# Attention and mixture-of-experts kernel: where VectorE adds the low-rank tiles to the weights of two experts

## The reference

```python
gate = jnp.einsum('btd,edf->ebtf', x, Wg)
up = jnp.einsum('btd,edf->ebtf', x, Wu)
gate = gate.at[:NL].add(jnp.einsum('btd,edr,erf->ebtf', x, Ga, Gb))
up = up.at[:NL].add(jnp.einsum('btd,edr,erf->ebtf', x, Ua, Ub))
mid = jax.nn.silu(gate) * up
out = jnp.einsum('ebtf,efd->ebtd', mid, Wd)
out = out.at[:NL].add(jnp.einsum('ebtf,efr,erd->ebtd', mid[:NL], Da, Db))
```

## Time and profile before

| what | value |
| --- | --- |
| median of 3 executions | 1037.57 us (1037.39 to 1037.73) |
| time of the profiled execution | 1037.73 us |
| its span, first to last instruction | 1036.0 us |
| TensorE busy | 1027.2 us, 99% |
| VectorE busy | 751.6 us, 73% |
| ScalarE busy | 458.3 us, 44% |
| granted TensorE clock | 1.000 over the whole span |

### The profile page before, as it was taken

The page is one execution under the profiler, slowest core; times in us unless marked ns, Lnnn a source line. Parts: engine busy times, 40 slices in busy tenths (PEclk is TensorE's granted clock), DMA queues, the critical chain, the costliest instruction groups (busy, mean ns, idle before and its releaser), DMA issues.

```text
span 1036.0 us, 12632 instructions
## 1 busy us (share of the span) xinstructions
PE 1027.2 (99%) x4663; PEld 846.0 (82%) x4663; DVE 751.6 (73%) x1266; ACT 458.3 (44%) x719; POOL 84.3 (8%) x115
## 2 busy tenths in 40 slices
PE   8999999999999999999999999999999999999998
PEld 6887787887888888888888888888888888888887
DVE  6888778877484865758577695986868586877664
ACT  6563354463443443435334344443536253534530
POOL 2611121101000000000100011000000000000000
PEclk9999999999999999999999999999999999999999
DMA  9410204348566473954848573536353544544342
GB/s 304 156 51 1 82 22 163 94 110 293 195 218 249 169 247 133 298 201 172 283 135 309 176 255 122 183 121 202 115 197 87 204 132 179 148 162 163 110 175 82
DMA packets 95709, 173.43 MB, mean 167 GB/s; under 512 B 5728, under 2 KB 62240, under 8 KB 94752
## 3 DMA queue, kind: packets, MB, share of 16 engines
q1 hardware_dynamic: 87584, 125.37, 37.2%
q0 software_dynamic: 7776, 47.19, 12.2%
q10 hardware_dynamic: 288, 0.07, 0.0%
HBM read 111.23 MB, written 61.37 MB: 167 GB/s over the span
## 4 chain that ended last, share of the span: by engine, by line
PE 91%; DVE 3%; issue 2%; ACT 2%; POOL 1%; DVEq 0%; ACTq 0%; POOLq 0%
PE gate_up L2177 17%; PE gate_up L2179 17%; PE gate_up L2178 17%; PE tiles L2024 7%; PE tiles L2025 7%; PE tiles L2023 7%; PE tiles L2197 4%; PE tiles L2196 4%; PE tiles L2195 4%; PE gate_up L2134 2%; PE gate_up L2135 2%; PE gate_up L2140 2%; ACT w_raw L893 1%; PE tiles L2166 0%; PE tiles L2165 0%
## 5 line engine op out<-in xcount | busy, mean ns | idle before, releaser
L2177 PE MATMUL gate_up<-xT_hi,piece_hi 128*128 128x512 f32 x448 | 174.7, 390 | 0.0
L2178 PE MATMUL gate_up<-xT_hi,piece_lo 128*128 128x512 f32 x448 | 174.3, 389 | 0.0
L2179 PE MATMUL gate_up<-xT_lo,piece_hi 128*128 128x512 f32 x448 | 174.3, 389 | 0.0
L2177 PE MATMUL gate_up<-tx_hi,piece_hi 128*128 128x512 f32 x336 | 131.1, 390 | 0.3
L2179 PE MATMUL gate_up<-tx_lo,piece_hi 128*128 128x512 f32 x336 | 130.8, 389 | 0.0
L2178 PE MATMUL gate_up<-tx_hi,piece_lo 128*128 128x512 f32 x336 | 130.7, 389 | 0.0
L1495 DVE TENSOR_TENSOR piece_lo<-piece,piece_hi 128x1024 fp32r<-128x1024 f32 x88 | 93.1, 1099 | 27.8 <-ACT piece_hi L1012 27.2
L1025 ACT ACTIVATE gate_up<-gate_up 128x512 f32<-128x512 f32 x56 | 32.6, 582 | 180.6 <-PE gate_up L2179 120.0
L2023 PE MATMUL tiles<-wd_hi,mids_hi 128*128 128x512 f32 x256 | 99.6, 389 | 0.0
L2025 PE MATMUL tiles<-wd_hi,mids_lo 128*128 128x512 f32 x256 | 99.6, 389 | 0.0
L2024 PE MATMUL tiles<-wd_lo,mids_hi 128*128 128x512 f32 x256 | 99.6, 389 | 0.0
(11 more groups left out here) (241 smaller groups left out, 1928.8 us busy)
## 6 DMA issues: line engine op xcount, KB each, us to landing
piece_spill<-piece_hi POOLq DMA_DIRECT2D x24, 896.0 KB, 4.5
piece_spill<-piece_lo POOLq DMA_DIRECT2D x24, 896.0 KB, 7.0
piece_hi<-piece_spill SPq DMA_DIRECT2D x24, 896.0 KB, 4.5
piece_lo<-piece_spill SPq DMA_DIRECT2D x24, 896.0 KB, 6.5
piece<-in_wg_dram SPq DMA_DIRECT2D x24, 256.0 KB, 4.4
piece<-in_wu_dram SPq DMA_DIRECT2D x24, 256.0 KB, 6.2
merged<-lora_w SPq DMA_DIRECT2D x6, 1024.0 KB, 6.2
wd_raw<-in_wd_dram SPq DMA_DIRECT2D x5, 1024.0 KB, 5.2
```

Source lines behind the costliest of these rows:

```text
L2177: nc.tensor.matmul(dst, w_h, x_h, start=first and kt == 0, stop=False, skip_group_check=True)
L2178: nc.tensor.matmul(dst, w_l, x_h, start=False, stop=False, skip_group_check=True)
L2179: ins = nc.tensor.matmul(dst, w_h, x_l, start=False, stop=last and kt == 1, skip_group_check=True)
```

## The change

For jobs 0 to 5 `add_lora(k)` no longer stands in step k between the low part of `wd` and the C21 product. It is called at the top of the next turn of VectorE's loop, behind the C22 sum of the second up piece and ahead of that piece's C11 product. The condition `k <= len(LORA_JOBS)` holds for the turns k = 1 to 6. No other engine's program changes.

```diff
--- before.py
+++ after.py
@@ -1823,6 +1823,8 @@
                 lora = k < len(LORA_JOBS)
                 if k > 0:
                     combine(k - 1, UP, 1, C22)
+                    if k <= len(LORA_JOBS):
+                        add_lora(k - 1)
                     make_mid(k - 1, 1, C11)
                     mid_low_part(k - 1, 1, C12)
                     make_mid(k - 1, 1, C22)
@@ -1922,8 +1924,6 @@
                 mid_low_part(k, 0, C22)
                 if k != 0:
                     wd_low_part(k)
-                if lora:
-                    add_lora(k)
                 if k != 0:
                     make_mid(k, 0, C21)
                 combine(k, UP, 1, C12)
```

## The result

The changed kernel takes 1040.33 us (median of 11 executions, 1040.06 to 1042.56) against 1037.38 us for the kernel before, run beside it (1036.59 to 1038.39). The ratio is 1.0033, with a 95% interval of 1.0025 to 1.0040. The forecast was 1040.6 us. The profiled execution is one of the two slowest of the eleven: 1042.53 us, of which 1040.8 are span. So its trace holds more than the median does, which has to be told apart.

What follows compares the result with a forecast made beforehand. TensorE, busy 1027.2 of 1036.0 us, was taken as the bound. Terms -0.1 (job 0), +2.8 (jobs 1 to 5) and +0.4 (SyncE's queue) gave +3.1 us: 1040.6 us predicted, range 1038.2 to 1044.5.

Steps and rivals of the forecast that it cites:

- Job 0: Adds leave the front of the C12 sum: 0.86 us of stalls become 0.77 at product 6, gaining 0.1 us.
- Jobs 1 to 5: Adds land behind the C22 sum's wait for product 7; ScalarE's copy delays product 6, 0.56 us each, 2.8 us.
- SyncE's queue: Later merged-weight store delays the base and piece loads behind it; 0.4 us taken, bounds 0 and 3.1 us.
- The first rival: In jobs 1 to 5 ScalarE's copy is in time, product 6 doesn't wait: 1036.7 to 1037.5 us; 0.23 including half.
- The second rival: Later loads meet the spill of piece 4k+1, product 4 of the second gate quad stalls: +5 to +9 us; chance 0.2.
- The third rival: The change reaches three jobs only, two of five stalls come: about +1.1 us, 1038.7 us; chance 0.02.

Runs made afterwards that it cites:

- the late store: Kernel before, with the store of a job's merged weights also waiting for the second up piece's C11 product: 1040.62 us (1037.05 to 1047.19), ratio 1.0032.
- the piece first: Kernel with all adds behind the C11 product, with SyncE loading piece 4k+2 ahead of store wait and base load: 1044.57 us, ratio 1.0053.

## Why the prediction was right, and where its terms were off

- **Job 0: right.** Both stalls of 0.86 us in all go, and product 6 waits in their place. Forecast 0.64 us and 0.1 us won; the start lost 0.63, and the kernel with job 0 alone is at 1.0000.
- **Jobs 1 to 5: right.** The forecast walked VectorE from 296.77 to a C11 product at 299.64 and a copy at 300.41; the trace has 296.73, 299.59 and 300.37. The loss was put at 0.43 + 0.13 us a job and is 0.46 + 0.13, 2.95 us for five against 2.8. The Trainium skill (VectorE: DVE Perf Modes, "The DRAIN you can't avoid") has the next instruction wait for an empty pipe, which would have been some 1.2 us more; the same section adds that a next one "that is not held starts earlier". The rows go with this addition, though no run here shows what holds an instruction: 0.68 us long, they start 0.60 apart here as well, and the measured sum doesn't leave room for 1.2 us.
- **SyncE's queue: the mechanism was right, its term was off.** The forecast counted 1.0 us won back by a store with the queue to itself; it was 1.9. The 0.4 us taken for product 4 in step 5 is not there: in the profile of an ordinary execution nothing stalls for the queue. The jobs cost 0.15 us more than forecast, which takes back part of it. That the sum of 3.1 came within 0.15 us of the measured 2.95 is in part luck; the stalls read from the trace make 2.85. Step 6 has no term in the forecast, whose walk through the queue ends at step 5, and it is the one that stalls when piece 26 is slow, by 1.85 us.
- **The first rival** (the copy in time) fell: five stalls, and they go exactly when the chain is made 0.54 us shorter, or when its first add is done in VectorE's idle time.
- **The second rival** (the transfers decide) is not this kernel's usual case, but its mechanism is real. It was given 5 to 9 us, and the neighbouring orders show executions up to 9.7 us above the kernel before. Why the changed kernel, with its store at the same time as those, mostly escapes it is not shown. A spill issued farther behind the piece load could be the reason: from the first load of piece 10 to the spill it is 2.5 us in the changed kernel and 1.3 with the adds behind the C11 product. But the late store has 2.3, hardly less than the changed kernel, and scatters; and in step 6 of the changed kernel the same 4.0 us went with a late load once and with none the other time.
- **The third rival** fell: all six jobs moved.

What stays open is why one load of a piece's two lands 3 us and more behind the other when a spill is issued around it, why it does so in some executions only, and what the slow executions with the late store look like; no run here shows it.

## What to carry to other kernels

When work is moved behind a later operation, ask what that operation waits for: behind a wait, the work no longer fills idle time and stands whole on the chain that follows. Walk from the wait to the next thing the busiest engine needs, subtract the room that is there, and do it for every repetition, since the one place with a stall to win (here job 0, 0.1 us) may differ from the five that pay (0.59 us each). A change that moves a store also moves every load behind it; where loads and spills are under way together, time many executions: here the profiled ones were now the fastest, now the slowest of a kernel.

## What the hardware showed that was not expected

- **A stall of 2.5 us cost the clock as well.** In the kernel with the adds behind the C11 product TensorE starts nothing from 319.06 to 321.82. The clock granted from 321.80 to 325.20 is 0.52 of full speed, so the lower level of 1.2 GHz, and matmuls start 0.43 us apart; from 325.20 it is 1.00 again. The stall of step 6 (3.1 us, from 570.42 to 573.72 without a start) was followed by 0.57 up to 577.70. The stalls of the changed kernel, 0.46 to 0.86 us, left the pitch at 0.227, and behind those of 1.1 and 1.4 us in the kernel with the piece first the granted clock stayed at 1.00.
- **One of two loads came late.** In step 2 a piece of two 256 KB loads could be used 6.6 us after its issue in the kernel before, where the spill was issued 4.1 us behind it, and 11.7 or 13.9 us when a spill was issued 1.3 us behind it or 1.0 us ahead of it. The distance alone doesn't decide, as step 6 of the changed kernel shows.
- **The same store took 6.16 us beside other transfers and 4.29 us a few microseconds later.** It was issued 4.0 us later and was over 2.1 us later.
- **A restart has a price.** Behind every stall of TensorE from 0.1 to 1.4 us in these runs the second matmul starts 0.11 us late: 0.33 or 0.34 us after the first in place of 0.227.
